# Attention over heads as a program of its own: sums ahead of the maximum, four slots of probabilities, rows normalised by ScalarE

## What is computed

```
def _L2_xattn_ref(Query, Key, Value, Wq, Wk, Wv, Wo):
    ...
    q = (Query @ Wq.T).reshape(b, -1, H, DK).transpose(0, 2, 1, 3)
    ...
    scores = jnp.einsum('bhqd,bhkd->bhqk', q, k) / jnp.sqrt(jnp.float32(DK))
    attn = jax.nn.softmax(scores, axis=1)
    ctx = jnp.einsum('bhqk,bhkd->bhqd', attn, v)
    ctx = ctx.transpose(0, 2, 1, 3).reshape(b, -1, H * DK)
    return ctx @ Wo.T
...
x = x + jnp.tanh(g_xattn[2]) * _L2_xattn_ref(_layernorm(x, axis=-1), ctx_1024, ctx_1024, ...)
```

## Time and profile before

| what | us |
|---|---|
| median of three runs | 1668.2 (1667.2 to 1670.81) |
| the profiled execution | 1669.93 |
| its span, first to last instruction | 1668.1 |
| TensorE busy | 1395.9 (84%) |
| VectorE busy | 1056.0 (63%) |
| GpSimd busy | 789.5 (47%) |
| ScalarE busy | 695.9 (42%) |
| the head-softmax phase, first to last start of its first head sum | 655.3 to 849.2 |

### The profile page before, as it was taken

How to read it: one execution, slowest core, us unless ns; L and a number is a source line. 1 busy time by engine, 2 the same in 40 slices (tenths; PEclk the granted TensorE clock), 3 DMA queues, 4 the chain that set the end, 5 groups by cost and what they waited for, 6 DMA issues and landing times. The chain is left out here.

```text
span 1668.1 us, 34024 instructions
## 1 busy us (share of the span) xinstructions
PE 1395.9 (84%) x10919; PEld 1117.9 (67%) x10919; DVE 1056.0 (63%) x2354; ACT 695.9 (42%) x1695; POOL 789.5 (47%) x1005
## 2 busy tenths in 40 slices
PE   4999774989656785999979986999999999687996
PEld 3777554989645454666645555787888787486984
DVE  4888761413389696999958883555565755263455
ACT  3676452323344332665544442445545544321121
POOL 2554581244275353455434441544544577207445
PEclk9999896999855797999979998999999999898898
DMA  7400015659210000000000000000000000375952
GB/s 185 181 1 2 11 31 157 204 170 268 76 37 13 1 1 1 1 0 0 0 1 0 0 0 1 1 0 0 1 1 1 10 15 18 89 218 176 285 155 84
DMA packets 96485, 100.02 MB, mean 60 GB/s; under 512 B 12149, under 2 KB 69677, under 8 KB 95726
## 3 DMA queue, kind: packets, MB, share of 16 engines
q1 hardware_dynamic: 62322, 69.60, 13.8%
q0 software_dynamic: 8192, 16.79, 3.3%
q10 hardware_dynamic: 25852, 12.09, 2.6%
HBM read 72.23 MB, written 26.21 MB: 59 GB/s over the span
## 5 line engine op out<-in xcount | busy, mean ns | idle before, releaser
L439 POOL TENSOR_TENSOR exp_scores<-exp_scores,softmax_recip 128x308 f32<-128x308 f32 x256 | 181.9, 743 | 180.7 <-DVE softmax_recip L611 180.6
L633 PE MATMUL psum<-identity,exp_scores 128*77 128x128 f32 x1024 | 163.6, 285 | 38.8 <-POOL exp_scores L439 26.2
L1944 POOL TENSOR_TENSOR exp_scores_xattn<-exp_scores_xattn,softmax_recip_xattn 128x1640 f32<-128x1640 f32 x32 | 93.5, 2923 | 162.4 <-DVE softmax_recip_xattn L2117 162.4
L1201 PE MATMUL psum<-sorted_transposed_ffn,tile_weights_up_ffn 128*128 128x128 f32 x1280 | 165.7, 284 | 5.3 <-DVE sorted_transposed_ffn L1089 5.2
L633 PEld LDWEIGHTS psum<-identity,exp_scores 128*77 128x77 f32 x1024 | 122.1, 152 | 61.9 <-issue 29.4
L1201 PEld LDWEIGHTS psum<-sorted_transposed_ffn,tile_weights_up_ffn 128*128 128x128 f32 x1280 | 155.1, 198 | 12.2 <-DVE sorted_transposed_ffn L1089 11.6
L975 POOL DMA_INDIRECT gathered_rows_ffn<-sorted_y,slot_ffn x96 | 90.9, 947 | 105.7 <-DMA sorted_y<-expert_rows_ffn 47.1
L454 ACT COPY probs_transposed<-psum 77x512 f32<-77x512 f32 x192 | 111.3, 582 | 57.3 <-PE psum L633 55.3
L964 POOL DMA_INDIRECT sorted_x<-xn_ffn,slot_ffn x64 | 61.5, 961 | 141.2 <-DVE slot_ffn L851 122.4
L1211 PE MATMUL psum<-expert_weights_down_ffn,hidden_ffn 128*128 x960 | 124.5, 281 | 3.4 <-issue 2.9
L1211 PEld LDWEIGHTS psum<-expert_weights_down_ffn,hidden_ffn 128*128 128x128 f32 x960 | 116.8, 197 | 5.3 <-issue 5.2
(11 more groups left out here) (367 smaller groups left out, 3373.9 us busy)
## 6 DMA issues: line engine op xcount, KB each, us to landing
tile_weights_up_ffn<-in_L_ffn_packed_dram SPq DMA_DIRECT2D x160, 256.0 KB, 3.2
sorted_rows_ffn<-sorted_x SPq DMA_DIRECT2D x80, 128.0 KB, 3.5
sorted_y<-expert_rows_ffn ACTq DMA_DIRECT2D x80, 128.0 KB
sorted_x<-zeros SPq DMA_DIRECT2D x4, 1280.0 KB, 13.2
x_residual<-in_x_dram SPq DMA_DIRECT2D x4, 512.0 KB, 11.0
expert_weights_down_ffn<-in_L_ffn_packed_dram SPq DMA_DIRECT2D x8, 256.0 KB, 14.0
sorted_x<-xn_ffn,slot_ffn POOLq DMA_INDIRECT x128, 2.2
gathered_rows_ffn<-sorted_y,slot_ffn POOLq DMA_INDIRECT x128, 2.7
```

Source lines behind the costliest of these rows:

```text
L439: nc.gpsimd.tensor_tensor(e[:, par, heads, :], e[:, par, heads, :], rec.to_broadcast([S, HG, KC]), ALU.mult).then_inc(s["probs_ready"], 1)
L633: last = nc.tensor.transpose(m.psum[0:KC, 4 + g % 2, h * S:(h + 1) * S], e[:, nxt, g * HG + h, :], m.ident[:, :])
L1201: mm = nc.tensor.matmul(m.psum[:, 2 * (n % 2) + half, to:to + SUB], w[:, n % DEPTH, u, at:at + 128], xst[:, n % 2, u * SUB:(u + 1) * SUB], ...
L1944: nc.gpsimd.tensor_tensor(ev, ev, recip[:, par, :].unsqueeze(2).to_broadcast([S, H3, KV]), ALU.mult).then_inc(s["probs_ready"], 1)
```

## The change

The third attention gets a function of its own, `attention_over_heads`, and its own `pipeline6`, which runs b from -1 to 34 (the steps 4 to 27 in a loop of four); `has(b, lag)` says whether batch b - lag exists. The first attention keeps `head_attention`.

Each engine's step is put in a new order. VectorE sums the exponentials of b-1 first, then takes the maximum of b, statistics, the keys of b+1, the probability copy of b-2, the reciprocal of b-1, and the update of x of b-3. GpSimd multiplies the probabilities of b-2 and then copies the context slot. The transposes belong to b-2 and the products with the values to b-3, one stage later than before; the exponentials and the padded values have four slots in place of two. TensorE makes the scores first, and the second group of transposes stands ahead of the subtraction of the maximum. ScalarE normalises the rows of b+2, first in its step, and copies the queries ahead of the values, after the value projection too. The rows of batch 0 are normalised by ScalarE behind the load of the exponential's table.

```
+    RING = 4
+        vpad = sb("v_padded", [KC, RING, HEADS, VPAD])
+        e = sb("exp_scores", [S, RING, HEADS, KC])
...
+                def step(b, ring):                                                  # GpSimd
+                    if has(b, 2):
+                        wait(pool, s["recip_ready"], b - 1)
+                        for g in range(NG):
+                            ev = e[:, (ring - 2) % RING, g * HG:(g + 1) * HG, :]
+                            nc.gpsimd.tensor_tensor(ev, ev, recip[:, ring % 2, :].unsqueeze(1).to_broadcast([S, HG, KC]),
+                                                    ALU.mult).then_inc(s["probs_ready"], 1)
+                    if has(b, -2):
+                        wait(pool, s["v_in_psum"], b + 1)
+                        nc.gpsimd.tensor_copy(cts[:, ring % 2, :], m.ctx_t[:, bass.ds((b + 2) * KC, KC)]).then_inc(s["ct_ready"], 1)
...
+                preload(nc, m, ACT.Exp)                                             # ScalarE
+                act.wait_ge(s["shift_ready"], 1)
+                def normalise(b, slot):
+                    nc.scalar.activation(xn[:, slot, :], m.x[:, b, :], ACT.Identity, scale=m.rstd[:, bass.ds(b, 1)],
+                                         bias=m.shift[:, bass.ds(b, 1)]).then_inc(s["xn_ready"], 1)
...
+                    if has(b, -2):
+                        wait(act, s["xt_in_psum"], b + 1)
+                        normalise(b + 2, par)
...
+                    if has(b, -1):
+                        wait(act, s["proj_in_psum"], b + 2)
+                        wait(act, s["v_in_psum"], b + 1)
+                        wait(act, s["scores_done"], b)
+                        nc.scalar.copy(qt[:, nxt, :], m.psum[:, 6, S:2 * S]).then_inc(s["q_ready"], 1)
...
+                def step(b, ring):                                                  # VectorE
+                    par, nxt = ring % 2, 1 - ring % 2
+                    if has(b, 1):
+                        ev = e[:, (ring - 1) % RING, :, :]
+                        wait(dve, s["exp_ready"], b)
+                        wait(dve, s["sum_ready"], b - 1)
+                        wait(dve, s["recip_ready"], b - 2)
+                        nc.vector.tensor_tensor(partial[:, 0:8, :], ev[:, 0:8, :], ev[:, 8:16, :], ALU.add).then_inc(s["half_sums"], 1)
+                        wait(dve, s["half_sums"], b * 3 - 2)
+                        nc.vector.tensor_tensor(partial[:, 8:12, :], partial[:, 0:4, :], partial[:, 4:8, :], ALU.add).then_inc(s["half_sums"], 1)
...
+                        nc.vector.tensor_tensor(total[:, nxt, :], partial[:, 12, :], partial[:, 13, :], ALU.add).then_inc(s["sum_ready"], 1)
+                    if has(b, 0):
+                        wait(dve, s["scores_done"], b + 1)
+                        wait(dve, s["shifted"], b - 1)
+                        nc.vector.tensor_reduce(negmax[:, par, :], m.psum[:, 0:NG, 0:HG * KC].rearrange("p j (h k) -> p k j h", k=KC), AX.XY,
+                                                ALU.max, negate=True).then_inc(s["negmax_ready"], 1)
+                    if has(b, 4):
+                        statistics(b - 4)
...
+                    if has(b, 1):
+                        wait(dve, s["sum_ready"], b)
+                        wait(dve, s["probs_ready"], (b - 2) * NG)
+                        nc.vector.reciprocal(recip[:, nxt, :], total[:, nxt, :]).then_inc(s["recip_ready"], 1)
+                    if has(b, 3):
+                        wait(dve, s["y_done"], b - 2)
+                        nc.vector.scalar_tensor_tensor(m.x[:, b - 3, :], m.psum[:, 7, S:2 * S], gate, m.x[:, b - 3, :],
+                                                       ALU.mult, ALU.add).then_inc(s["x_done"], 1)
...
+                def step(b, ring):                                                  # TensorE: scores(b), transposes(b-2, group 0),
...
+                    if has(b, 2):                                                   # rows b+1, values b-3, projections, then
+                        transposes(b, ring, 1)
+                    if has(b, 0):
+                        wait(pe, s["negmax_ready"], b + 1)
...
-            phase(head_attention, 2, (m.wq2, m.wk2, m.wv2, m.wo2), None)
+            phase(attention_over_heads, (m.wq2, m.wk2, m.wv2, m.wo2))
```

165 lines of the change are left out of this document (added).

## The result

The changed kernel takes 1695.59 us (median, 1693.93 to 1696.48) against 1668.09 for the kernel before in the same comparison: a ratio of 1.0164, 95% interval 1.0151 to 1.0177, slower by 27.5 us. 1702 was forecast, with 1682 to 1736 as the range. The profiled execution took 1695.35, its span is 1693.6.

The account below looks back on a forecast made before the run. VectorE, hardly ever idle, was taken to bound the phase's 6.22 us step. One step of 5.6 and thirty of 7.28 make 224.0 against 193.9, +30.1; with +0.85 and +2.7, +33.7 on 1668.2: 1702 us, range 1682 to 1736.

Parts of the forecast that it names:

- The collision: VectorE's head sums and GpSimd's products take turns in every step; sums done 4.13 us after the reciprocal, step 7.28; 66%.
- the remainder: Rest of the step after the head sums: maximum, keys, copy, reciprocal and statistics, 3.15 us.
- price of a delayed product: A GpSimd product held up by a head sum costs 0.65 us, its median of 0.78 less 0.13.
- In that gap a pending product goes in: Each head sum waits by a semaphore for the one before; a GpSimd product enters there, hand-overs 0.04 us each.
- The rival in which three sums pass behind one product: First head sum waits for one product, the other three pass: step 5.87, 1658 us; part of the faster rival, 14%.
- the slower one: Rival: the first head sum waits for all four products; step 8.1, 1727 us; chance 17%.
- The part that gains: Step without a collision: 5.41 us (VectorE) to 5.6 (TensorE), whole kernel 1643 to 1649 us; faster rival, 14%.
- the ring: Loop without a collision: shift, exponential, scores, transposes, 5.6 us a step; in the kernel before: maximum, shift, exponential, sums, reciprocal.
- Waits added: New waits of the query copy and TensorE's new order cost nothing in the step; TensorE has 1.6 us to spare.
- Start and end: Outside the phase's steady steps: first normalisation behind ScalarE's table load +0.85 us, last batch's sums and reciprocal +2.7.
- +33.7 in the sum: Whole phase: 31 steps +30.1 us, start +0.85, end +2.7.
- The signs that the prediction gives for a bound left out: In the phase: a copy of the queries ending after the maximum, or a clock below full speed.

Follow-up runs that it names:

- a1: The changed kernel with each of GpSimd's four products cut to one of 77 keys, most of the normalisation left out: 1658.3 us, ratio 0.9940.
- a4: The changed kernel with eight GpSimd products of two heads instead of four of four: 1683.3 us, 1.0086 against the kernel before.
- a3: The changed kernel with GpSimd's four products made one product of sixteen heads: 1725.6 us, 1.0336 against the kernel before.
- d1: The changed kernel with the first head sum cut into two halves that do not wait for each other: 1701.9 us, 1.0190 against the kernel before.
- a2: The changed kernel with the four head sums replaced by one reduction with one SBUF input: 1658.4 us, 0.9939 against the kernel before.
- b1: The changed kernel with the reciprocal back ahead of the maximum, and GpSimd's products with it: 1666.2 us, 0.9980 against the kernel before.
- b3: The kernel before with its four head sums replaced by one reduction, no product beside it: 1679.5 us, 1.0057 against the kernel before.

## Why the prediction was right, step by step

*The collision.* Forecast and found, in every step. Its sizes: the sums were to be done 4.13 us after the reciprocal, and are at 4.07 (743.53 to 747.60); the remainder was 3.15 and is 3.06; the step 7.28, and 7.13. The sums were to take about 1.3, 1.0, 0.8 and 0.75 us and have medians of 1.19, 0.95, 0.79 and 0.70; the products' median was to rise from 0.78 to about 1.0, and their mean from 680 to 865 us is 1.00 (their median, 0.94, since the first of the four is not held up). The first sum is shorter than forecast because it doesn't ask 0.2 after the reciprocal but 0.40 (743.93), when 0.32 of the first product's 0.79 is over: it waits 0.23 for the exponential, which ends with a late shift. That wait was no term of the sum, and the forecast needed it. With the exponential in time the sum asks 0.08 after the reciprocal and not 0.2, together with the product, and then it often goes first: in 12 of 21 steps of a1 and 15 of 19 of a4, from 695 to 825 us. In the changed kernel the exponential is 0.15 to 0.34 late in every step of that stretch, and the product goes first in each. So that four products stand among the sums and not three was right for a reason that the prediction didn't give. With three, the sums would be done about 0.65 sooner, by the prediction's own price of a delayed product (an estimate; no run with four whole products shows it).

*What of it is turn and what is bandwidth.* That was argued from rows of other phases; a3 and d1 show it here: one instruction at a time, alternately.

*The mechanism within it.* "In that gap a pending product goes in" was wrong as a cause, right as a count of turns. d1 shows that a product gets in without a gap. The rival in which three sums pass behind one product (1658 us) fell with it; and the slower one, in which the first sum waits for all the products, is what a3 makes.

The turns don't always alternate, though, and the trace of before shows it. In the competitive attention VectorE's L1477, with two SBUF inputs of up to 308 elements, asks while GpSimd's L1356 runs, and loses its turn to L1360 as well:

```profile
490.30 1.05 POOL L1356 TENSOR_TENSOR weighted_tokens_xattn<-xn_xattn,best_sim_xattn 128x512 f32<-128x512 f32 x1
...
490.52 2.17 DVE L1477 TENSOR_TENSOR pick_xattn<-pick_xattn,pick_code_xattn 128x308 f32<-128x308 f32 x1
...
491.30 1.04 POOL L1360 TENSOR_TENSOR gated_xn_xattn<-xn_xattn,tanh_gates 128x512 f32<-128x512 f32 x1
```

It ends at 492.69, 0.35 after the second GpSimd operation; at 466.26 and 478.31 the same line ends 0.34 after the second of the two. That is what the slower rival needs, and the prediction had only L1475's 2295 ns for it. Why VectorE gets in between any two products of the changed kernel and not between these two operations is open, so that the forecast had the order of turns right is in part luck.

*The part that gains.* 5.41 to 5.6 without a collision was forecast; a1 and a2 show 5.8, with TensorE as the bound. The 5.6 was 0.2 short because TensorE's own work fills the step (59.53 of 60 us), not the ring that I summed; the rival times that rest on 5.41 and 5.6 (1643 and 1649) were out of reach by the same number.

*Waits added.* TensorE waits 1.27 us ahead of the shift, as said, so the added waits cost nothing here. a4 shows that this cover is thin: with the sums done 1.5 us sooner, TensorE's wait for the products takes over.

*Start and end.* The phase, from its first variance operation to its last statistics, took 859.1 - 643.6 = 215.5 us before and takes 893.4 - 646.8 = 246.6, as the first and the last of its lines in the timeline show:

```profile
646.79 0.21 DVE L316 TENSOR_TENSOR x_mean_doubled<-x_moments 128x32 f32<-128x32 f32 x1 [0.31 <-PEq L1812]
...
893.10 0.29 DVE L866 BATCH_NORM_STATS2 x_moments<-x_residual 128x6 f32<-128x128 f32 x1
```

That is +31.1, against +33.7 in the sum. The loop: first sums from 659.3 to 879.3, 220.0, so +26.1 against the +30.1 of the sum; the 0.15 that the step is shorter, thirty times, is 4.5, and the first step took 0.5 more than forecast (6.14). The signs that the prediction gives for a bound left out are both there: the granted clock is 0.50, its lower level, from 650 to 670 us (in the kernel before 0.60 to 0.72 from 650 to 665, then 1.00), and the copy of the queries ends at 663.53, after the maximum's end at 662.62. The start: 12.5 against 11.6 us from the variance to the first sum, +0.9, near the forecast +0.85, but by another path. The first normalisation begins 0.77 later, and of that 0.26 is left at the first maximum (7.98 us after the variance instead of 7.72). Then the shift begins 0.82 later, since in the new order it stands on TensorE behind the projections of the next batch, at the low clock. The size was luck. The end: 14.1 against 9.9 us from the last first sum on, +4.2 where +2.7 was forecast. The two parts that were costed make 2.1 (879.33 to the reciprocal's start at 883.40, 4.07 instead of 1.96). The other 2.1 were forgotten: from the last reciprocal to the last statistics it takes 10.0 us instead of 7.9, since in the deeper order TensorE has the head products of batch 30 (885.59) and its output projection (887.79) to do between the transposes of batch 31.

*From the phase to the whole.* The whole became 27.5 us longer, less than the phase's 31.1. The phase began 3.2 us later in the profiled execution of after, and what follows it was 8.8 shorter (1693.6 - 893.4 against 1668.1 - 859.1). None of that code was changed; and in the ten profiled executions of this study the start of the phase, behind the same code, lies between 642.0 and 646.8 us, and what follows the phase takes 800.2 to 809.0. So some 5 us ahead of the phase and 9 behind it are scatter of a single execution, and a comparison of two spans can't carry a difference of that size; the medians and the phase by itself can. The forecast of 1702 was 6 us too high. Of these, 2.6 lie in the phase (33.7 against 31.1); the rest lies between the phase of the two profiled executions and the medians, within the scatter just named.

## What to carry to other kernels

A move that frees an engine on paper also moves whatever that instruction triggers: the reciprocal left the ring (0.3 us a step, from b1's 6.10 to the 5.8 of a1 and a2), and its four products landed on the sums (1.32). Before moving such a step, list what each triggered operation will run beside, and look in the trace for the same pair of engines with two SBUF inputs on VectorE: if one of them ends only after the other there, cost the pair as turns, instruction by instruction, ask which of them comes first, and take for the upper end that VectorE loses more than one turn in a row. Where the pair can't be pulled apart, look for a form of the work that doesn't collide, even a slower one: here a reduction of 2.29 us for sums of 1.99 turned a loss of 1.6% into a gain of 0.6%.

## What the runs showed of the hardware

- In the changed phase a VectorE sum of two SBUF inputs and a GpSimd product of SBUF data alternate in every step, also where VectorE's next sum waits for nothing: 1058 ns instead of 480 (d1). If both ask together, either can go first: the sum in 12 of 21 steps of a1 and 15 of 19 of a4. In the changed kernel, a3 and d1 the sum asks at least 0.1 us after the product, and it waited for it in every step from 695 to 825 us.
- In another phase of the kernel before, a VectorE instruction of two SBUF inputs waited for two GpSimd instructions in a row (L1477 behind L1356 and L1360, 2.17 us at 490.52).
- A VectorE reduction of one SBUF input beside the same products: 2326 ns against 2287 alone, the products 787 against 782 in b1 (a2, b3). That it is the second SBUF input that makes the sums take turns, and not their operation, was not tried apart from this; L548 shows that one input is no safeguard for every operation.
- The reduction over heads 77 elements apart takes 2.29 us for 1232 elements in SBUF; the maximum over as many elements, read from PSUM, takes 1.43. That the difference is due to the memory, and not to the operation or the order of the elements, was not tried.
- GpSimd's products of 1232, 308 and 154 elements take 2.58, 0.78 and 0.44 us at the least, so cutting one in half saves 43%: shorter turns cost extra time in total.
